# First transfers of an attention and feed-forward kernel chained one behind the other, with the first stage's order changed on all engines

## The chip, the cores and the metric

The chip is a Trainium2. The program handles one batch entry of 2048 tokens on one core; the input has eight entries, so the same program runs on the chip's eight cores at once, each with its own copy of the weights to load. The metric is the device time of the slowest core in microseconds.

## The reference

```python
xn = _layernorm(x)                                   # x: [8, 2048, 1024]
qkv = xn @ W_attn + b_attn                           # 16 heads of 64
att = q @ k.T / sqrt(64) / temperature + alibi_bias  # causal
y = softmax(att) @ v;  attn = y @ W_proj + b_proj
gate, up = xn @ wg.T, xn @ wu.T                      # hidden size 3072, int32 weights / 127
ffn = (silu(gate) * up) @ wd.T
out = x + attn + ffn
```

## The kernel before

The work has three parts: a first stage that normalises x, transposes it and makes V and the first head pair's q and k; a long middle stage (attention woven with gate and up); and the output stage. The change touches the first and a few waits around it.

x has 16 tiles of 128 tokens. For tile i, SP loads it into one of four buffers `xstage` (lines 339 to 343; from the fifth tile on it waits until the tile that held the buffer is normalised, semaphore `v_xn`). The vector engine takes statistics (two `bn_stats` and a `bn_aggr`, line 499), ScalarE the square root `sd` (line 624), the vector engine the reciprocal `rs` and the normalised tile `xn_st` (line 507). PE transposes it with eight 128-column matmuls into PSUM, in turn `ps_s` and `ps_gu` (line 742). ScalarE copies that to `xnT` (line 631). Below, Ti is the transpose of tile i and xi the tile itself.

A V unit is one tile times one half of the V weights: eight matmuls of 512 columns from `xnT` and `wv_b` into one of two halves of `ps_t` (line 767), copied by ScalarE to `Vt` (line 639). There are 32 units, numbered here in PE's order: V0, V1 and so on. The table `v_at` sets that order: half 0 of the first four tiles, then half 1 of the same four, then both halves of each tile. A q or k group is eight matmuls of 512 columns for four tiles (line 707). q of head pair 0 is taken from `ps_m` by the vector engine (`evac_q`, line 474), k from `ps_y` by ScalarE (`evac_k`, line 600). The loop index i of each engine's stream carries several tiles at once: PE transposes tile i and makes V of tile i-1; ScalarE takes the root of tile i, copies the transposed tile i-2 and V of tile i-3.

The orders are written out by hand per engine, with semaphores between engines. Transfers go through two queues: x on SP's (q1), weights that are cast from float32 or int32 to bf16 while they move on POOL's (q0). POOL waits for x0 and x1, then issues the V weights of half 0 (2 MB read), the weights of the first q/k pair (1 MB) and the V weights of half 1 (2 MB) without a wait between them (lines 403 to 409), then runs twelve memsets for constant rows of `qx` and `kx` (lines 410 to 418). After the twelfth tile is normalised it issues the first gate and up weights, the next pair's q/k weights and W_proj.

Of the kernel before, what the change touches and what calls it, by code (L numbers as in the profile page):

```python
# [11 lines left out]
I32 = mybir.dt.int32  # L12
# [7 lines left out]
DC = C // 128  # L20
# [25 lines left out]
    "v_t", "v_cbq", "v_ln", "v_xn", "v_q", "v_mx", "v_mc", "v_rc", "v_y", "v_h", "v_out",  # L46
# [101 lines left out]
def build_program(T):  # L148
    NT = T // 128
# [26 lines left out]
    with st:  # L176
# [93 lines left out]
        v_at = {i: [(i - 1, 0)] for i in range(1, 5)}  # L270
        v_at[4] += [(tt, 1) for tt in range(4)]
        for i in range(5, NT + 1):
            v_at[i] = [(i - 1, 0), (i - 1, 1)]
        V0 = {i: sum(len(v_at[k]) for k in v_at if k < i) for i in range(NT + 3)}
# [40 lines left out]
        def _(e):  # L315
# [34 lines left out]
            for k, (_, t, _, M) in enumerate(steps):  # L350
                if M is not None and M[0] == "qk" and M[2]:
                    p, u = M[1] // 8 + 1, M[1] % 8
                    if u == 0:
                        if p >= 2:
# [37 lines left out]
        def _(e):  # L392
# [29 lines left out]
            cast_qk(1)  # L422
            e.dma_start(out=wpj_b[:, :], in_=wproj_r[:, :]).then_inc(sem["l_wp"], 16)
# [45 lines left out]
        def _(e):  # L469
# [21 lines left out]
            for i in range(NT + 1):  # L491
                if i < NT:
                    b = i % 4
                    e.wait_ge(sem[f"l_x{b}"], 16 * (i // 4 + 1))
                    for k in range(2):
                        e.bn_stats(st6[b][:, 6 * k:6 * k + 6], xstage[b][:, k * 512:(k + 1) * 512]).then_inc(  # L496
                            sem["v_ln"], 1)
                    e.wait_ge(sem["v_ln"], 4 * i + 1 if i else 2)
                    e.bn_aggr(mv[b][:, :], st6[b][:, :]).then_inc(sem["v_ln"], 1)
                if i:  # L500
                    b = (i - 1) % 4
                    e.wait_ge(sem["a_sd"], i)
                    e.reciprocal(rs[b][:, :], sd[b][:, :]).then_inc(sem["v_ln"], 1)
                    e.wait_ge(sem["v_ln"], 4 * i + (3 if i < NT else 0))
                    if i > 4:
                        e.wait_ge(sem["p_xT"], i - 4)
                    e.tensor_scalar(xn_st[b][:, :], xstage[b][:, :], mv[b][:, 0:1], rs[b][:, :],
                                    AluOpType.subtract, AluOpType.mult).then_inc(sem["v_xn"], 1)
                if i == 1:
                    e.wait_ge(sem["l_const"], 16 * 4)  # L510
                    e.tensor_scalar(t8_s[0:1, :], temp_s[0:1, :], 8.0, None, AluOpType.mult).then_inc(
                        sem["v_t"], 1)
                    e.wait_ge(sem["v_t"], 2)
                    e.reciprocal(c11_s[0:1, :], t8_s[0:1, :]).then_inc(sem["v_t"], 1)
                if i == 5:
                    e.wait_ge(sem["a_c"], 1)
                    e.tensor_scalar(cbq_s[:, :], bqk_s[:, 0:8], cvec_s[:, :], None, AluOpType.mult).then_inc(
                        sem["v_cbq"], 1)
                    e.wait_ge(sem["v_cbq"], 1)
                if i >= 6 and i % 4 == 2:  # L520
                    evac_q(0, i // 4 - 1)
# [73 lines left out]
        def _(e):  # L595
# [21 lines left out]
            e.wait_ge(sem["v_t"], 1)  # L617

            V3 = Vt.rearrange("p (g d) -> p g d", d=VW)
            for i in range(NT + 3):  # L620
                if i < NT:
                    b = i % 4
                    e.wait_ge(sem["v_ln"], 4 * i + 2 if i else 3)
                    e.activation(sd[b][:, :], mv[b][:, 1:2], AF.Sqrt, bias=eps_s[:, :]).then_inc(sem["a_sd"], 1)
                if i == 4:
                    e.wait_ge(sem["p_c"], 1)
                    e.activation(cvec_s[:, :], ps_m[:, 0:1], AF.Copy).then_inc(sem["a_c"], 1)
                if 2 <= i < NT + 2:
                    k = i - 2
                    e.wait_ge(sem["p_xT"], k + 1)  # L630
                    e.activation(xT3[:, :, k * 128:(k + 1) * 128],
                                 (ps_gu if k % 2 else ps_s).rearrange("p (d t) -> p d t", d=DC),
                                 AF.Copy).then_inc(sem["a_xe"], 1)
                for x, (tt, half) in enumerate(v_at.get(i - 2, [])):
                    n = V0[i - 2] + x
# [6 lines left out]
                    if i == 6 and x == 0:  # L642
                        evac_k(0, 0)
                if i >= 11 and i % 4 == 3:
                    evac_k(0, i // 4 - 1)
# [55 lines left out]
        def _(e):  # L701
# [33 lines left out]
            e.wait_ge(sem["l_id"], 16)  # L735
            for i in range(NT + 2):
                if i < NT:
                    e.wait_ge(sem["v_xn"], i + 1)
                    if i >= 2:
                        e.wait_ge(sem["a_xe"], i - 1)  # L740
                    for dc in range(DC):
                        mm = e.matmul((ps_gu if i % 2 else ps_s)[:, dc * 128:dc * 128 + 128],
                                      xn_st[i % 4][:, dc * 128:(dc + 1) * 128], ident_s[:, :],
                                      start=(dc % 4 == 0), stop=(dc % 4 == 3))
                    mm.then_inc(sem["p_xT"], 1)
                if i == 3:
                    e.wait_ge(sem["v_t"], 3)
                    e.wait_ge(sem["l_const"], 16 * 4)
                    e.matmul(ps_m[:, 0:1], onesf_s[0:1, :], c11_s[0:1, :], start=True, stop=True).then_inc(
                        sem["p_c"], 1)  # L750
                for x, (tt, half) in enumerate(v_at.get(i, [])):
                    n = V0[i] + x
                    e.wait_ge(sem["a_xe"], tt + 1)
                    if i == 1:
                        e.wait_ge(sem["l_wv0"], 16)
                    if i == 4 and x == 1:

                        e.wait_ge(sem["a_xe"], 4)
                        e.wait_ge(sem["l_wq0"], 16)
                        e.wait_ge(sem["a_c"], 1)  # L760
                        q_or_k(0, 0, ps_m, range(DC)).then_inc(sem["p_qk"], 1)
                        q_or_k(0, 1, ps_y, range(DC)).then_inc(sem["p_qk"], 1)
                        e.wait_ge(sem["l_wv1"], 16)
                    if n >= 2:
                        e.wait_ge(sem["a_v"], n - 1)
                    for dc in range(DC):
                        mm = e.matmul(ps_t[:, n % 2 * 512:n % 2 * 512 + 512],  # L767
# [224 lines left out]
```

## Time and profile before

| | us |
|---|---|
| runs of the kernel | 1156.03, 1156.49, 1157.23; median 1156.49 |
| profiled execution, device time | 1156.21 |
| its span (slowest core, core 4) | 1154.7 |
| spans of the eight cores | 1150.5 to 1154.7 |
| first gate/up matmul of core 4 | 113.88 |

The profile was taken on the slowest core. The span goes from the first to the last instruction; the device time also holds what lies around it (1.5 us). Times inside are from the span's start. A row of the chain of waits says how long the end of the program hung on that piece; a row of the timeline says when an instruction or a run of like ones started, how long it took, and in brackets how long its engine had been idle and who released it. PE is the matmul engine, DVE the vector engine, ACT ScalarE, POOL GpSimd.

### The profile page before, as it was taken

Reading aid. Unit: us, or ns where it says so; the run is one execution under the profiler, and the core shown is the slowest. Engines: PE = TensorE matmul, PEld = TensorE weight load, DVE = VectorE, ACT = ScalarE, POOL = GpSimd, SP = SyncE. Lnnn points to the kernel's source line nnn. Section 1 sums busy time; section 2 is a strip of 40 time slices with the busy share of each in tenths; the row PEclk is TensorE's granted clock in tenths of the full one; section 3 lists DMA queues with packets and bytes.
Section 4 is the critical chain, followed back from the end, with each engine's and each line's share of the span. In section 5 each row is a group of like instructions: output and inputs, shape, how many; then the busy total and the mean of one; then the engine's idle time right before and its main releaser. Section 6 shows DMA issues by size and latency. Waiting matters only on the chain.

```text
span 1154.7 us, 24726 instructions; the slowest of 8 cores (1150.5 to 1154.7 us)
## 1 busy us (share of the span) xinstructions
PE 1107.8 (96%) x7830; PEld 569.8 (49%) x7830; DVE 586.5 (51%) x1190; ACT 531.3 (46%) x965; POOL 267.2 (23%) x289
## 2 busy tenths in 40 slices
PE   2898999999999999999999999999999999999998
PEld 1344455555555555555555555555555344444443
DVE  5441866766666766676666666666773100000110
ACT  1443456655755665565566566556667300000000
POOL 7210122222221222122222112112223432121221
PEclk9899999999999999999999999999999999999999
DMA  9439041333312333133311312112420652525222
GB/s 188 126 95 179 12 80 41 75 66 70 74 29 62 78 62 65 38 74 67 69 38 24 67 33 52 31 31 56 165 56 20 217 189 73 182 73 182 73 73 73
DMA packets 39648, 94.19 MB, mean 82 GB/s; under 512 B 5876, under 2 KB 26485, under 8 KB 38438
## 3 DMA queue, kind: packets, MB, share of 16 engines
q0 software_dynamic: 7872, 35.66, 16.1%
q1 hardware_dynamic: 28770, 48.45, 13.5%
q10 hardware_dynamic: 2884, 8.50, 1.9%
q8 instruction: 71, 1.16, 0.4%
q14 instruction: 51, 0.42, 0.1%
HBM read 90.49 MB, written 27.26 MB: 102 GB/s over the span
## 4 chain that ended last, share of the span: by engine, by line
PE 88%; DVE 5%; issue 3%; DMA 2%; ACT 1%; POOL 1%; DVEq 0%; ACTq 0%; POOLq 0%; SPq 0%
PE ps_gu L727 25%; PE ps_dn L895 14%; PE ps_s L818 10%; PE ps_t L799 10%; PE ps_m L707 9%; PE ps_y L834 5%; PE ps_dn L890 5%; PE ps_t L767 5%; DVE cm L548 3%; DMA xstage<-xin 2%; PE ps_m L847 1%; PE ps_s L821 1%; PE ps_t L803 1%; PE ps_m L855 1%; DVE st L496 1%
## 5 line engine op out<-in xcount | busy, mean ns | idle before, releaser
L548 DVE TENSOR_REDUCE cm<-ps_s 128x1 f32<-128x512 f32 (+3 forms) x640 | 380.1, 608 | 198.5 <-PE ps_s L818 105.0
L656 ACT ACTIVATE pt<-ps_t 128x512 bf16<-128x512 f32 (+1 forms) x576 | 327.3, 575 | 222.3 <-PE ps_t L799 134.2
L727 PE MATMUL ps_gu<-xnT,wubuf 128*128 128x512 bf16 x768 | 261.9, 378 | 2.1 <-DVE hst L484 1.7
L727 PE MATMUL ps_gu<-xnT,wgbuf 128*128 128x512 bf16 x768 | 261.3, 378 | 1.2 <-ACT kst L600 1.2
L818 PE MATMUL ps_s<-kx,qx 67*128 67x512 bf16 (+3 forms) x640 | 213.1, 347 | 10.4 <-DVE cm L548 9.1
L799 PE MATMUL ps_t<-qx,kx 98*128 98x512 bf16 (+3 forms) x640 | 216.4, 348 | 1.5 <-ACT pt L656 1.2
L426 POOL TENSOR_SCALAR th_s<-th_s 128x512 f32<-128x512 f32 x96 | 59.4, 618 | 626.0 <-ACT th_s L608 626.0
L895 PE MATMUL ps_dn<-wdres,hb 128*128 128x512 bf16 x768 | 168.5, 379 | 0.0
L834 PEld LDWEIGHTS ps_y<-Vt,pt 128*128 128x128 bf16 x2176 | 125.4, 97 | 82.0 <-issue 0.4
L834 PE MATMUL ps_y<-Vt,pt 128*128 128x65 bf16 x2176 | 138.9, 193 | 0.0
L589 DVE SCALAR_TENSOR_TENSOR outsb<-ps_dn,xres 128x512 f32<-128x512 f32 x32 | 20.7, 687 | 205.3 <-PE ps_dn L895 205.3
L707 PE MATMUL ps_m<-xnT,wqk_b 128*128 128x512 bf16 x480 | 122.9, 380 | 0.0
L895 PEld LDWEIGHTS ps_dn<-wdres,hb 128*128 128x128 bf16 x768 | 75.2, 98 | 90.6
L432 POOL TENSOR_TENSOR gs_s<-th_s,gh_s 128x512 bf16<-128x512 f32 x96 | 111.0, 1156 | 26.4 <-POOL th_s L426 26.4
L818 PEld LDWEIGHTS ps_s<-kx,qx 67*128 67x128 bf16 x640 | 61.8, 97 | 94.3 <-issue 41.3
L727 PEld LDWEIGHTS ps_gu<-xnT,wubuf 128*128 128x128 bf16 x768 | 73.0, 98 | 57.4 <-issue 5.8
L727 PEld LDWEIGHTS ps_gu<-xnT,wgbuf 128*128 128x128 bf16 x768 | 73.5, 98 | 52.7 <-issue 1.7
L484 DVE SCALAR_TENSOR_TENSOR hst<-ps_gu,gs_s 128x512 bf16<-128x512 f32 x96 | 65.7, 684 | 41.4 <-POOL gs_s L432 31.3
L799 PEld LDWEIGHTS ps_t<-qx,kx 98*128 98x128 bf16 x640 | 62.5, 98 | 30.5 <-issue 5.1
L608 ACT ACTIVATE th_s<-ps_gu 128x512 f32<-128x512 f32 x96 | 57.1, 595 | 29.5 <-PE ps_gu L727 28.9
L767 PE MATMUL ps_t<-wv_b,xnT 128*128 128x512 bf16 x256 | 62.2, 399 | 4.2 <-DMA wv_b<-wv_r 2.7
L707 PEld LDWEIGHTS ps_m<-xnT,wqk_b 128*128 128x128 bf16 x480 | 41.8, 98 | 38.9 <-issue 1.2
(77 smaller groups left out, 793.1 us busy)
## 6 DMA issues: line engine op xcount, KB each, us to landing
h_sc<-hst SPq DMA_DIRECT2D x96, 128.0 KB, 1.7
hb<-h_sc SPq DMA_DIRECT2D x4, 3072.0 KB, 14.1
xstage<-xin SPq DMA_DIRECT2D x16, 512.0 KB, 6.3
xres<-xin POOLq DMA_DIRECT2D x16, 512.0 KB, 4.6
out<-outsb ACTq DMA_DIRECT2D x15, 512.0 KB, 2.7
wgbuf<-wg_r POOLq DMA_DIRECT2D x12, 512.0 KB, 6.4
wubuf<-wu_r POOLq DMA_DIRECT2D x12, 512.0 KB, 9.1
wd_sc<-wd_r POOLq DMA_DIRECT2D x12, 512.0 KB, 8.3
```

Source lines behind the costliest of these rows:

```text
L426: e.tensor_scalar(th_s[f % 2][:, :], th_s[f % 2][:, :], 1.0, 1.0, AluOpType.add, AluOpType.mult).then_inc(sem["g_th"], 1)
L432: e.tensor_tensor(gs_s[f % 2][:, :], th_s[f % 2][:, :], gh_s[f % 2][:, :], AluOpType.mult).then_inc(sem["g_s"], 1)
L484: e.scalar_tensor_tensor(hst[f % 4][:, :], ps_gu[:, 512:1024], 1.0 / 127.0, gs_s[f % 2][:, :], AluOpType.mult, AluOpType.mult).then_inc(se ...
L548: e.tensor_reduce(cm[:, c0:c0 + 1], ps_s[:, s % 2 * 512:s % 2 * 512 + w], AX.X, AluOpType.max, negate=True).then_inc(sem["v_mx"], 1)
L656: e.activation(pt[t % NPT][:, 0:w], ps_t[:, t % 2 * 512:t % 2 * 512 + w], AF.Exp).then_inc(sem["a_e"], 1)
L707: mm = e.matmul(ps[:, :], wqk_b[p % 2][:, f0 + dc * 256:f0 + dc * 256 + 128], xnT[:, dc * T + tc * 512:dc * T + (tc + 1) * 512], start=(dc ...
L727: mm = e.matmul(ps_gu[:, r // 8 * 512:r // 8 * 512 + 512], w[:, w0:w0 + 128], xnT[:, dc * T + tb * 512:dc * T + tb * 512 + 512], start=(dc ...
L767: mm = e.matmul(ps_t[:, n % 2 * 512:n % 2 * 512 + 512], xnT[:, dc * T + tt * 128:dc * T + (tt + 1) * 128], wv_b[:, half * 4096 + dc * 512: ...
L799: mm = e.matmul(ps_t[:, c0 + off:c0 + off + w], k_[0:KT, kt * 128:(kt + 1) * 128], q_[0:KT, b * 512 + i0 * 128:(b + 1) * 512], start=(x == ...
L818: mm = e.matmul(ps_s[:, r0:r0 + w], q_[0:KS, b * 512 + i * 128:b * 512 + (i + 1) * 128], k_[0:KS, c0:c0 + w], start=True, stop=not diag)
L834: mm = e.matmul(ps_y[:, i * VW:(i + 1) * VW], pt[a % NPT][:, c0:c0 + 128], Vt[:, (kt * H + h) * VW:(kt * H + h + 1) * VW], start=(T0[n] == ...
L895: return e.matmul(ps_dn[:, r0:r0 + 512], hb[tb % 2][:, hc * 512 + ts * 128:hc * 512 + ts * 128 + 128], wdres[:, hc * 1024 + half * 512:hc ...
```

## The change

SP issues x0 and x1 at once, x2 and x3 when the first quarter of the V weights (`l_wva`) has landed, x4 when x2 has landed, x5 when x4 has landed, x6 when all V weights have landed, and the rest as before. POOL fills the constant rows of pair 0 first, now written as 32-bit words, half as many elements; it issues the first quarter of the V weights after x0, the second after x1, the q/k weights after the second quarter has landed, the third quarter after x3, the fourth after the q/k weights. The memsets for pair 1 go behind the weight transfers after the twelfth tile. V units are taken in another order (half 0 of six tiles, half 1 of the same six, then both halves tile by tile), q/k groups and transposes stand elsewhere, and ScalarE runs a root on a constant ahead of its first real one. The vector engine's single counter `v_ln` becomes three.

```diff
@@ sync @@
             for i in range(NT):
+                if i == 2:
+                    e.wait_ge(sem["l_wva"], 16)
+                if i == 4:
+                    e.wait_ge(sem["l_x2"], 16)
+                if i == 5:
+                    e.wait_ge(sem["l_x0"], 32)
+                if i == 6:
+                    e.wait_ge(sem["l_wv1"], 32)
                 if i >= 4:
                     e.wait_ge(sem["v_xn"], i - 3)
                 e.dma_start(out=xstage[i % 4][:, :], in_=xin[i * 128:(i + 1) * 128, :]).then_inc(
                     sem[f"l_x{i % 4}"], 16)
-            e.wait_ge(sem["g_set"], 13)
+            e.wait_ge(sem["g_set"], 7)
@@ gpsimd @@
+            def set_rows(q, k):
+                for j in range(2):
+                    e.wait_ge(sem["g_set"], k + 3 * j)
+                    e.memset(qx[q][j][64:96, :].bitcast(I32), 0x3F803F80).then_inc(sem["g_set"], 1)
+                    e.wait_ge(sem["g_set"], k + 3 * j + 1)
+                    e.memset(kx[q][j][64:96, :].bitcast(I32), 0).then_inc(sem["g_set"], 1)
+                    e.wait_ge(sem["g_set"], k + 3 * j + 2)
+                    e.memset(kx[q][j][96:98, :].bitcast(I32), 0x3F803F80).then_inc(sem["g_set"], 1)
             e.memset(Vt.rearrange("p (g d) -> p g d", d=VW)[:, :, 64:65], 1.0).then_inc(sem["g_set"], 1)
+            set_rows(0, 1)
             e.wait_ge(sem["l_x0"], 16)
+            e.dma_start(out=wv_b[:, 0:2048], in_=wv_r[0, :, 0:2048]).then_inc(sem["l_wva"], 16)
             e.wait_ge(sem["l_x1"], 16)
-            for half in range(2):
-                e.dma_start(out=wv_b[:, half * 4096:(half + 1) * 4096], in_=wv_r[half, :, :]).then_inc(
-                    sem[f"l_wv{half}"], 16)
-                if half == 0:
-                    cast_qk(0)
...
+            e.dma_start(out=wv_b[:, 2048:4096], in_=wv_r[0, :, 2048:4096]).then_inc(sem["l_wvb"], 16)
+            e.wait_ge(sem["l_wvb"], 16)
+            cast_qk(0)
+            e.wait_ge(sem["l_x3"], 16)
+            e.dma_start(out=wv_b[:, 4096:6144], in_=wv_r[1, :, 0:2048]).then_inc(sem["l_wv1"], 16)
+            e.wait_ge(sem["l_wq0"], 16)
+            e.dma_start(out=wv_b[:, 6144:8192], in_=wv_r[1, :, 2048:4096]).then_inc(sem["l_wv1"], 16)
             e.wait_ge(sem["v_xn"], NT - 4)
             cast_gu(0)
             cast_gu(1)
             cast_qk(1)
+            set_rows(1, 7)
+            e.wait_ge(sem["g_set"], 13)
             e.dma_start(out=wpj_b[:, :], in_=wproj_r[:, :]).then_inc(sem["l_wp"], 16)
@@ vector, from tile 6 on @@
+            for i in range(6, NT):
+                if i + 1 < NT:
+                    statistics(i + 1)
+                normalise(i)
+                if i % 4 == 1:
                     evac_q(0, i // 4 - 1)
             evac_q(0, NTB - 1)
@@ scalar @@
             e.wait_ge(sem["v_t"], 1)
+            e.activation(sd[3][:, :], eps_s[:, :], AF.Sqrt)
...
+            for i in range(6, NT):
+                if i + 1 < NT:
+                    evac_x(i + 1)
+                evac_v(2 * i, 2 * i + 1)
+                if i + 2 < NT:
+                    deviation(i + 2)
+                evac_v(2 * i + 1, 2 * i + 2)
+                if i % 4 == 0:
                     evac_k(0, i // 4 - 1)
@@ tensor @@
+            transpose_x(0)
+            transpose_x(1)
+            values(0, 2)
+            transpose_x(2)
+            transpose_x(3)
...
+            values(2, 4)
+            first_qk(0)
+            transpose_x(4)
+            transpose_x(5)
+            values(4, 6)
+            e.wait_ge(sem["l_wv1"], 32)
+            values(6, 10)
+            transpose_x(6)
+            values(10, 12)
+            for i in range(6, NT):
+                if i + 1 < NT:
+                    transpose_x(i + 1)
+                values(2 * i, 2 * i + 2)
+                if i % 4 == 3:
+                    first_qk(i // 4)
```

**PE, first stage.** `wv_b` is the V weights, `ident_s` the transposing identity, `wqk_b` the q/k weights. A row is a run of like matmuls with their count; eight on `ps_t` are one V unit. Before, from T1 to the first four units of half 1:

```order
L742 MATMUL ps_gu<-ident_s,xn_st 128x128 x8
L767 MATMUL ps_t<-wv_b,xnT 128x512 x8
L742 MATMUL ps_s<-ident_s,xn_st 128x128 x8
L767 MATMUL ps_t<-wv_b,xnT 128x512 x8
L742 MATMUL ps_gu<-ident_s,xn_st 128x128 x8
L749 MATMUL ps_m<-c_s,onesf_s 128x1
L767 MATMUL ps_t<-wv_b,xnT 128x512 x8
L742 MATMUL ps_s<-ident_s,xn_st 128x128 x8
L767 MATMUL ps_t<-wv_b,xnT 128x512 x8
L707 MATMUL ps_m<-xnT,wqk_b 128x512 x8
L707 MATMUL ps_y<-xnT,wqk_b 128x512 x8
L767 MATMUL ps_t<-wv_b,xnT 128x512 x32
```

And now:

```order
L804 MATMUL ps_gu<-ident_s,xn_st 128x128 x8
L820 MATMUL ps_t<-wv_b,xnT 128x512 x16
L804 MATMUL ps_s<-ident_s,xn_st 128x128 x8
L804 MATMUL ps_gu<-ident_s,xn_st 128x128 x8
L846 MATMUL ps_m<-c_s,onesf_s 128x1
L820 MATMUL ps_t<-wv_b,xnT 128x512 x16
L771 MATMUL ps_m<-xnT,wqk_b 128x512 x8
L771 MATMUL ps_y<-xnT,wqk_b 128x512 x8
L804 MATMUL ps_s<-ident_s,xn_st 128x128 x8
L804 MATMUL ps_gu<-ident_s,xn_st 128x128 x8
L820 MATMUL ps_t<-wv_b,xnT 128x512 x48
```

Transposes now come in twos with two units behind them, T4 and T5 stand behind the first q/k groups, and six units follow these without a break; the wait for the second half's weights has moved from the fifth unit to the seventh.

**POOL, start of the program.** Before:

```order
L402 MEMSET Vt 128x256
L406 DMA wv_b<-wv_r 128x4096 [waits l_x0,l_x1]
L395 DMA wqk_b<-wqk_r 128x2048
L406 DMA wv_b<-wv_r 128x4096
L414 MEMSET qx 32x2048 [waits g_set]
L416 MEMSET kx 32x2048 [waits g_set]
L418 MEMSET kx 2x2048 [waits g_set]
```

Now:

```order
L422 MEMSET Vt 128x256
L416 MEMSET qx 32x1024 [waits g_set]
L418 MEMSET kx 32x1024 [waits g_set]
L420 MEMSET kx 2x1024 [waits g_set]
L425 DMA wv_b<-wv_r 128x2048 [waits l_x0]
L427 DMA wv_b<-wv_r 128x2048 [waits l_x1]
L405 DMA wqk_b<-wqk_r 128x2048 [waits l_wvb]
L431 DMA wv_b<-wv_r 128x2048 [waits l_x3]
L433 DMA wv_b<-wv_r 128x2048 [waits l_wq0]
```

Six memsets moved ahead of the first weight transfer and are half as long, and each later weight transfer waits for an earlier transfer.

**ACT, the loop from tile 6 on.** Before, one turn of the loop and the next:

```order
L624 ACTIVATE sd<-mv,eps_s 128x1 [waits v_ln]
L631 ACTIVATE xnT<-ps_s 128x8x128 [waits p_xT]
L639 ACTIVATE Vt<-ps_t 128x8x64 [waits p_v] x2
L624 ACTIVATE sd<-mv,eps_s 128x1 [waits v_ln]
L631 ACTIVATE xnT<-ps_gu 128x8x128 [waits p_xT]
L639 ACTIVATE Vt<-ps_t 128x8x64 [waits p_v] x2
```

Now:

```order
L663 ACTIVATE xnT<-ps_gu 128x8x128 [waits p_xT]
L673 ACTIVATE Vt<-ps_t 128x8x64 [waits p_v]
L658 ACTIVATE sd<-mv,eps_s 128x1 [waits v_ag]
L673 ACTIVATE Vt<-ps_t 128x8x64 [waits p_v]
L663 ACTIVATE xnT<-ps_s 128x8x128 [waits p_xT]
L673 ACTIVATE Vt<-ps_t 128x8x64 [waits p_v]
L658 ACTIVATE sd<-mv,eps_s 128x1 [waits v_ag]
L673 ACTIVATE Vt<-ps_t 128x8x64 [waits p_v]
```

The root (L658, before L624) stood ahead of the copy of a transposed tile and of both V copies; now it stands between the two V copies.

## Rows read from the trace of the kernel before

**Rows 1.** The page, busy time per engine: us, share of the span, instructions.

```profile
PE 1107.8 (96%) x7830; PEld 569.8 (49%) x7830; DVE 586.5 (51%) x1190; ACT 531.3 (46%) x965; POOL 267.2 (23%) x289
```

**Rows 2.** Chain that ended last, 0 to 110 us: start, us, what.

```profile
1.06 5.73 DMA xstage<-xin
...
17.23 14.70 DMA xstage<-xin
...
44.31 6.91 PE ps_t L767 x32
51.22 0.45 PE ps_gu L742 x8
51.67 3.45 PE ps_t L767 x16
```

**Rows 3.** Timeline of PE: start us, us, what, count [idle before, releaser].

```profile
21.00 3.42 PE L767 MATMUL ps_t<-wv_b,xnT 128*128 128x512 bf16 x8 [2.69 <-DMA wv_b<-wv_r]
...
76.17 0.61 PE L742 MATMUL ps_s<-ident_s,xn_st 128*128 128x128 bf16 x8 [2.00 <-ACT xnT L631]
...
113.88 0.38 PE L727 MATMUL ps_gu<-xnT,wgbuf 128*128 128x512 bf16 x1 [1.25 <-ACT kst L600]
```

**Rows 4.** Timeline of POOL, first 15 us.

```profile
2.26 1.25 POOL L402 MEMSET Vt<- 128x256 bf16 x1
...
8.95 0.54 POOL L406 DMA_DIRECT2D wv_b<-wv_r  x1 [5.45 <-DMA xstage<-xin]
...
10.60 1.80 POOL L414 MEMSET qx<- 32x2048 bf16 x1
...
14.80 1.80 POOL L418 MEMSET kx<- 2x2048 bf16 x1
```

**Rows 5.** Timeline of DVE and ACT: one tile beside memsets, then a steady turn.

```profile
10.53 2.42 DVE L507 TENSOR_SCALAR xn_st<-xstage,mv,rs 128x1024 bf16<-128x1024 f32 x1
...
51.32 0.60 ACT L639 ACTIVATE Vt<-ps_t 128x512 bf16<-128x512 f32 x1 [1.13 <-PE ps_t L767]
...
51.81 0.29 ACT L624 ACTIVATE sd<-mv,eps_s 128x1 f32<-128x1 f32 x1
...
52.20 0.16 DVE L503 RECIPROCAL rs<-sd 128x1 f32<-128x1 f32 x1 [4.63 <-ACT sd L624]
52.54 0.81 DVE L507 TENSOR_SCALAR xn_st<-xstage,mv,rs 128x1024 bf16<-128x1024 f32 x1 [0.18 <-DVE rs L503]
53.27 1.28 DVE L496 BATCH_NORM_STATS2 st<-xstage 128x6 f32<-128x512 f32 x2
...
54.65 0.21 DVE L499 BATCH_NORM_AGGREGATE mv<-st 128x2 f32<-128x12 f32 x1
```

**Rows 6.** Tiles: x from 10 to 22 us, x from 36 to 62 us, wgbuf throughout.

```profile
L342 SPq DMA_DIRECT2D xstage<-xin x3: 327/328/328, 13.0 to 19.7; - x3
...
DMA to landing us min/median/max: 10.8/14.7/14.8
...
DMA to landing us min/median/max: 3.4/3.4/3.7
...
DMA to landing us min/median/max: 6.0/6.4/15.0
```

**Rows 7.** DMA queues, 0 to 60 us: packets, MB, share of 16 engines.

```profile
q1 hardware_dynamic: 1838, 6.74, 34.8%
q0 software_dynamic: 576, 2.62, 29.7%
```

**Rows 8.** Windows: PE, PEld, DVE, ACT, POOL busy, granted clock, DMA share, GB/s.

```profile
21.00:24.50 3.50, 3.50 (x13) 1.37 (x14) 0.54 (x1) 0.00 (x0) 3.26 (x3) 1.00 1.15 224
30.00:34.00 4.00, 2.94 (x8) 0.89 (x8) 1.48 (x4) 0.54 (x2) 3.76 (x3) 0.62 0.89 279
```

**Rows 9.** Spans and granted clock of cores.

```profile
core 0: 1150.5 us, clock 0.998
...
core 4: 1154.7 us, clock 0.995
```

More of the change, by code:

```diff
@@ L267, in gu_of @@
             return (f // 4, f % 4) if f < NF_ATT else (f // 8 * 2 + f % 2, f % 8 // 2)
[L270 to L274, printed above, removed]
+        v_units = [(tt, 0) for tt in range(6)] + [(tt, 1) for tt in range(6)]
+        v_units += [(tt, half) for tt in range(6, NT) for half in range(2)]
         FM = [NF_ATT * 16 * (k + 1) // len(steps) for k in range(len(steps))]
@@ L353, in _ @@
                     if u == 0:
[L354 removed]
+                        if p == 1:
+                            e.wait_ge(sem["g_set"], 13)
+                        else:
                             e.wait_ge(sem["p_t"], pair_done(p - 2))
@@ L489, in _ @@
             e.memset(nm[1][:, :], 0.0).then_inc(sem["v_t"], 1)
[L491 to L520, printed above, removed]
@@ L617, in _, with deviation, evac_x, evac_v @@
             e.wait_ge(sem["v_t"], 1)
+            e.activation(sd[3][:, :], eps_s[:, :], AF.Sqrt)
             V3 = Vt.rearrange("p (g d) -> p g d", d=VW)
[L620 to L635, printed above, removed]
+            def deviation(i):
+                e.wait_ge(sem["v_ag"], i + 1)
+                e.activation(sd[i % 4][:, :], mv[i % 4][:, 1:2], AF.Sqrt, bias=eps_s[:, :]).then_inc(
+                    sem["a_sd"], 1)
+            def evac_x(i):
+                e.wait_ge(sem["p_xT"], i + 1)
+                e.activation(xT3[:, :, i * 128:(i + 1) * 128],
+                             (ps_gu if i % 2 else ps_s).rearrange("p (d t) -> p d t", d=DC),
+                             AF.Copy).then_inc(sem["a_xe"], 1)
+            def evac_v(n0, n1):
+                for n in range(n0, n1):
+                    tt, half = v_units[n]
                     e.wait_ge(sem["p_v"], n + 1)
@@ L641, in _ @@
                                  AF.Copy).then_inc(sem["a_v"], 1)
-                    if i == 6 and x == 0:
-                        evac_k(0, 0)
-                if i >= 11 and i % 4 == 3:
+            deviation(0)
+            deviation(1)
+            evac_x(0)
+            evac_x(1)
+            deviation(2)
+            evac_v(0, 1)
+            deviation(3)
+            evac_v(1, 2)
+            evac_x(2)
+            evac_x(3)
+            e.wait_ge(sem["p_c"], 1)
+            e.activation(cvec_s[:, :], ps_m[:, 0:1], AF.Copy).then_inc(sem["a_c"], 1)
+            evac_v(2, 4)
+            deviation(4)
+            evac_k(0, 0)
+            deviation(5)
+            evac_x(4)
+            evac_x(5)
+            evac_v(4, 9)
+            deviation(6)
+            evac_v(9, 10)
+            deviation(7)
+            evac_x(6)
+            evac_v(10, 12)
+            for i in range(6, NT):
[6 more added lines that the diff above has]
+                if i % 4 == 0:
                     evac_k(0, i // 4 - 1)
@@ L733, in gate_up, with transpose_x, values @@
                         mm.then_inc(sem["p_u"], 1)
[L735 to L752, printed above, removed]
-                    e.wait_ge(sem["a_xe"], tt + 1)
[L754 to L763, printed above, removed]
+            def transpose_x(i):
+                e.wait_ge(sem["v_xn"], i + 1)
+                if i >= 2:
+                    e.wait_ge(sem["a_xe"], i - 1)
+                for dc in range(DC):
+                    mm = e.matmul((ps_gu if i % 2 else ps_s)[:, dc * 128:dc * 128 + 128],
+                                  xn_st[i % 4][:, dc * 128:(dc + 1) * 128], ident_s[:, :],
+                                  start=(dc % 4 == 0), stop=(dc % 4 == 3))
+                mm.then_inc(sem["p_xT"], 1)
+            def values(n0, n1):
+                for n in range(n0, n1):
+                    tt, half = v_units[n]
+                    e.wait_ge(sem["a_xe"], tt + 1)
                     if n >= 2:
```

75 lines of the change are left out of this document (60 added, 15 removed), and 2 rows, old and new, of the table SEMS.

## The prediction

> **What bounds the kernel now.** I began with the busy shares: PE works 96% of the span, everything else about half [rows 1]. A saving must therefore shorten PE's path, and the change touches only the first stage (layer norm, transposes, V, first q/k pair). So I next read the chain that ended last, for that stage alone [rows 2]. Until 44.3 us it hops from a transfer of x to the vector engine to a few matmuls; the piece of 14.70 us waits for one tile of x. From 44.31 us it is nearly all PE: eight matmuls of a V unit take 1.73 us (3.45 for two), eight transposes 0.45. The timeline of PE [rows 3] has the rest: the first V unit waits for its weights until 21.00 us, PE stops for 2.00 us at 76.17 (and again at 97.58), and the first gate/up matmul, where the next stage begins, starts at 113.88 us. That instant is my yardstick: the 1040.8 us behind it keep their order on every engine, so I move the end by as much as the yardstick moves.
>
> The work ahead of it is 16 transposes, 32 V units and 8 q or k groups: 16 x 0.45 + 40 x 1.73 = 76.4 us. PE is thus without useful full-speed work for 37.5 us. Before 44.31 it did only 5 transposes, 4 V units and 2 groups (12.6 us). From there 11 transposes, 28 units and 6 groups are left, 63.8 us; with two stops of 2.0 that is 67.8, against 68.3 to the end of the last group. I keep the 0.5 as friction. The last group is followed by 1.25 us of waiting for its copy.
>
> **Part 1, POOL: memsets first, weights in parts.** The row initialisation for the first head pair (6 memsets) now stands ahead of the first weight transfer. Vt's memset ends at 3.51. A memset of 2048 bf16 values costs 1.8 us whether it covers 32 partitions or 2 [rows 4], so the price goes by the length of a row, and the new ones write rows of 1024 words. The trace has no word memset: by elements it is 0.9 us, by bytes 1.8. I take 0.9, as the cost per element of the nearest row, plus 0.11 for the step between two: 6 x 1.01 = 6.1, so the first weights are issued at 9.6 us instead of 8.95 (with bytes: at 15.0). The Trainium skill ("VectorE: DVE Perf Modes", section "Zero memsets can be issued as uint32 (trn2)") says a memset costs a cycle per element whatever the type; it says so of the vector engine only, and no row here shows it for POOL. Beside POOL's memsets the normalising pass took 2.42 us against 0.81 [rows 5]; now its first two fall after them. The activation table's load also leaves the chain. So both first tiles are transposed by about 13.5 us, but PE then waits for weights anyway: this gains nothing.
>
> **Part 2, the transfers.** Prices: a 512 KB tile of x alone lands 3.4 us after issue, but 10.8 to 14.8 us after it with the weight queue full; a transfer of a weight part's size (1 MB read, 512 KB written) lands 6.0 to 6.4 us after issue [rows 6]. Engine time: queue q1 moved 6.74 MB in 34.8% of 60 us, so a tile costs 1.63 us; queue q0 wrote 2.62 MB in 29.7%, so a part costs 3.56 us [rows 7]. Behind weights tile 4 landed at 13.0 + 10.8 = 23.8, tile 5 at 17.2 + 14.7 = 31.9: 8.1 us for 1.63 us of work, so x gets about 0.2 of the engines there. Of a part's 6.2 us, 2.6 are not engine time; half before the data, half behind, I get: wva lands at 15.9; wvb 19.7; x2 (issued at 16.0) 20.9; x3 23.6; wq0 27; x4 31.8; wv1 complete 35.2; x5 (issued when x4 has landed) 36.4; x6 39. In total the engines are no less busy than before, but about 3 us are lost between x1 and wva.
>
> **What the chain costs.** A lone tile's 3.4 us less its 1.63 leaves 1.8 us per link, exposed only where the other queue is empty. The Trainium skill ("DMA: Bandwidth & Descriptors", section "Anatomy of one DMA") speaks against chaining: about 2.0 us fixed per transfer, mostly the receipt. By 2.0 in place of 1.8, four links (wva, x2, x4, x5) would be 0.8 us dearer.
>
> **Part 3, PE's order.** From landing to transpose: statistics 1.38, aggregate and hop 0.30, sd to rs 0.39, rs to xn 0.34, xn 0.81, hop 0.13: 3.35 us [rows 5]. x2 (20.9) is normalised by 24.1, x3 behind it by 27.3; T3 runs at 27.4 and V2 behind it and the small product for the temperature at 28.3. The first matmuls after idling run 512 columns in 427 ns, the lower level of 1.2 GHz, though the granted clock of that stretch reads 1.00; later the grant itself fell to 0.62 after PE had idled [rows 3, 8]. I charge V2 3.4 us: V2 to 31.7, V3 33.4, q and k 36.9, T4 37.35. T5 waits for x5: 36.4 + 3.35 = **39.75**. Then T5 0.45 and V4 to V9 10.4: 50.6 us. The first unit that needs wv1, V6, comes at 43.7, and wv1 is there at 35.2.
>
> **Part 4, the steady loop.** Removed: both stops of 2.00 us, since the vector engine now takes q out of PSUM after the norm that PE needs. Added: ACT's square root for tile i+2 stands behind the copy of V unit 2i. From the end of that unit: copy starts 0.10 later (51.22 to 51.32), sd 0.49 later, rs 0.39, xn 0.34 + 0.81, hop 0.14 = 2.27 us [rows 2, 5]; PE has only the unit of 1.73 to cover it. So T6, T8, T10, T11, T12, T14, T15 come 0.54 us late (T9 and T13 have q/k groups as cover, T7 two more units): 7 x 0.54 = 3.8. The bounds are 0 (copy and root overlap better) and 7 x 0.8. The second pair's six memsets now run beside tiles 12 and 13, whose normalising may take 2.4 instead of 0.8; 13 is covered, I charge 1.0 (0 to 1.6).
>
> **Sum.** 50.6 + 0.54 (T6) + ten transposes, 22 units, 6 groups 52.9 + six late transposes 3.2 + memsets 1.0 + friction 0.5 + 1.25 = **110.0 us**, against 113.88: 3.9 us less. The profiled execution took 1156.21 us (span 1154.7), 0.28 below the median of the runs; 1156.2 - 3.9 gives 1152.3, and **1152.4** beside the median. A difference below 0.2% (2.3 us) can't be told from none. The cheap parts together: sources of statistics split over three semaphores, the earlier waits for 7 instead of 13, and the wpj load behind memsets cost nothing: the work that waits on them is tens of us away.
>
> **Rivals.**
> A. *The late transposes don't happen.* ACT's copy and root overlap, and x5's link is shorter by about 1 us. For it: after a copy the root starts before the copy's end [rows 5]. Against it: my 2.27 already has that overlap. It would give 110.0 - 3.8 - 1 = 105.2, or 1147.6.
> B. *Memsets cost by bytes.* Weights are issued at 15.0, 5.4 us later, and wva gates x2 and all behind: 115.4, or 1157.7, no change. The same comes out if the slowest core is set otherwise: the spans reach from 1150.5 to 1154.7 us [rows 9], and a core with a low grant early on could give back the 3.9.
> C. *Slower: x4 and x5 in series behind weights.* x5 is issued only when x4 has landed. The yardstick is x5's landing plus 73.6, so from a landing after 42.6 us on the kernel is measurably slower. If x4 takes the 14.7 us that a tile took behind a full weight queue [rows 6], it lands at 35.7, and x5 at its own 8.1 lands at 44: 117.6, or 1159.9. For it: the row. Against it: wv1's last part should be through by 35 us, after which a tile takes 3.4.
> D. *The change doesn't start earlier*: all of the gain would vanish if T2 to V3 ran at the low clock throughout; 3.5 more gives 1156.
>
> **Chances.** Forecast 0.48 (own range 1149 to 1154.1), A 0.22, B 0.12, C 0.10, D 0.08. Faster: the forecast and A, with a little of B and D, 0.72; same 0.18; slower 0.10. The range takes in nearly all of A and all of B, and leaves C out: 1146.6 to 1158.0.
>
> **What the new profile would show.** Right: the first weight transfer issued at 9 to 10 us, word memsets of about 0.9 us; x3 landing at 23 to 24, T5 near 40, wv1 waited for by nobody; no stop of 2.0 us beside q/k groups, but transposes of the loop waiting about 0.5 us for xn; the first gate/up matmul near 110. Wrong: memsets of 1.8 us (B); tiles four and five taking over 8 us each (C); PE without a wait between V units from 50 us on (A).

## The result, and the profile after

The changed kernel takes 1159.80 us (median of 7 runs, 1159.53 to 1160.92), the kernel before, run beside it, 1156.58. The ratio is 1.0030 with a 95% interval of 1.0019 to 1.0041: slower by about 3.4 us, where 4 us less had been forecast. The profiled execution took 1159.6 us. Now and then an execution of any of these kernels runs at a lower granted clock on one die and takes longer; the ratios leave those out.

Cores, of the changed kernel:

```profile
core 1: 1154.7 us, clock 0.997
...
core 4: 1158.0 us, clock 0.998
```

All eight spans lie between these two; before they went from 1150.5 to 1154.7 [rows 9]. So it is not one unlucky core. One execution of each kernel is profiled, on all eight cores; where nothing else is said, lines are those of its slowest core (core 4 for both kernels).

The yardstick, and what PE waited for, in the timeline of PE (start us, us, what [idle before, releaser]):

```profile
17.80 1.86 PE L820 MATMUL ps_t<-wv_b,xnT 128*128 128x512 bf16 x4 [4.85 <-DMA wv_b<-wv_r]
24.92 5.28 PE L820 MATMUL ps_t<-wv_b,xnT 128*128 128x512 bf16 x12 [5.26 <-DMA wv_b<-wv_r]
...
46.06 0.61 PE L804 MATMUL ps_gu<-ident_s,xn_st 128*128 128x128 bf16 x8 [3.23 <-DVE xn_st L525]
...
66.44 0.61 PE L804 MATMUL ps_s<-ident_s,xn_st 128*128 128x128 bf16 x8 [0.73 <-DVE xn_st L525]
...
117.66 0.38 PE L791 MATMUL ps_gu<-xnT,wgbuf 128*128 128x512 bf16 x1 [1.25 <-ACT kst L634]
```

The first gate/up matmul, the forecast's yardstick, starts at 117.66 instead of 113.88 us [rows 3]; the 1040.3 us behind it are as long as before (1040.8). So the yardstick held and everything is decided in the first stage. The half unit at 17.80 and the rest at 24.92 wait for the two weight parts; T5 starts at 46.06, where 39.75 was forecast.

The chain that ended last, for the first 60 us (start, us, what):

```profile
2.27 1.26 POOL Vt L422
...
3.64 0.96 POOL qx L416
...
9.86 7.80 DMA wv_b<-wv_r
17.70 0.04 issue
17.74 8.30 DMA xstage<-xin
...
26.17 6.12 DMA xstage<-xin
...
32.41 10.00 DMA xstage<-xin
...
42.50 1.30 DVE st L512 x2
```

Before, the chain ran through one tile of x (14.70 us) [rows 2]. Now it is POOL's memsets, then four transfers in series, wva, x2, x4, x5, 32.2 us together. Nothing but waits holds them in that order. How busy the transfer engines were (columns: PE, PEld, DVE, ACT, POOL busy, granted clock, DMA share, GB/s):

```profile
6.00:12.00 6.00, 1.08 (x10) 0.87 (x11) 3.78 (x11) 0.71 (x3) 4.92 (x6) 1.00 0.16 23
12.00:24.00 12.00, 2.81 (x12) 1.11 (x12) 0.09 (x1) 1.93 (x2) 0.00 (x0) 1.00 0.96 157
24.00:27.00 3.00, 2.08 (x5) 0.74 (x6) 0.87 (x2) 0.00 (x0) 0.53 (x1) 1.00 0.34 74
27.00:39.00 12.00, 10.19 (x44) 4.71 (x43) 5.71 (x13) 4.16 (x8) 1.06 (x2) 0.86 0.98 177
```

wva and wvb are the first and second part of the first half of the V weights. There are two holes: from 6 to 12 us the share is 0.16, because x0 and x1 have landed and POOL is still at its memsets (5.0 us of the engines unused); from 24 to 27 it is 0.34, because the q/k weights wait for wvb and x4 for x2, and both land at nearly the same time (2.0 us). The clock plays no part in either: the grant is 1.00, as it was in the first 30 us before.

The memsets, and the loop's turn from the copy of a V unit on:

```profile
3.64 0.94 POOL L416 MEMSET qx<- 32x1024 int32 x1
...
86.34 0.94 POOL L416 MEMSET qx<- 32x1024 int32 x1
87.41 1.38 POOL L418 MEMSET kx<- 32x1024 int32 x1
```

```profile
61.65 0.61 PE L804 MATMUL ps_gu<-ident_s,xn_st 128*128 128x128 bf16 x8
...
64.08 0.60 ACT L673 ACTIVATE Vt<-ps_t 128x512 bf16<-128x512 f32 x1 [0.66 <-PE ps_t L820]
64.58 0.28 ACT L658 ACTIVATE sd<-mv,eps_s 128x1 f32<-128x1 f32 x1
64.97 0.16 DVE L520 RECIPROCAL rs<-sd 128x1 f32<-128x1 f32 x1 [3.33 <-ACT sd L658]
65.38 0.81 DVE L525 TENSOR_SCALAR xn_st<-xstage,mv,rs 128x1024 bf16<-128x1024 f32 x1 [0.25 <-DVE rs L520]
```

The words cost by elements, 0.94 against 1.80 us [rows 4]; why the one at 87.41 took 1.38 is not explained; it ran beside the normalising of tile 12 (87.09 to 87.90). In the loop the root waits for the copy of V12, as forecast, and T8 follows at 66.44, 4.79 us behind T7 where a turn without a stop takes 3.90.

### The profile page after: what moved, and what is told of

Its sections match the earlier page's. It is cut to its first block, busy times and chain, and to the rows that moved or that the text cites. A ratio compares the mean times of both kernels' runs of the same rounds, so it can differ in the third digit from the quotient of the medians.

```text
span 1158.0 us, 24758 instructions; the slowest of 8 cores (1154.7 to 1158.0 us)
## 1 busy us (share of the span) xinstructions
PE 1108.6 (96%) x7830; PEld 569.5 (49%) x7830; DVE 582.1 (50%) x1190; ACT 532.8 (46%) x966; POOL 257.5 (22%) x291
## 4 chain that ended last, share of the span: by engine, by line
PE 87%; DVE 5%; issue 3%; DMA 3%; POOL 1%; ACT 1%; DVEq 0%; ACTq 0%; POOLq 0%; SPq 0%
PE ps_gu L791 25%; PE ps_dn L980 14%; PE ps_s L903 10%; PE ps_t L884 10%; PE ps_m L771 9%; PE ps_y L919 5%; PE ps_dn L975 5%; PE ps_t L820 3%; DVE cm L582 2%; DMA xstage<-xin 2%; PE ps_m L932 1%; PE ps_s L906 1%; PE ps_t L888 1%; DMA wv_b<-wv_r 1%; PE ps_m L940 1%
## 5 line engine op out<-in xcount | busy, mean ns | idle before, releaser
L642 ACT ACTIVATE th_s<-ps_gu 128x512 f32<-128x512 f32 x96 | 57.1, 595 | 29.4 <-PE ps_gu L791 28.9
```

## The experiments

Each time stands beside runs of the kernel before on the same chip, so the ratios compare. "First gate/up" is the mean over the eight cores of the yardstick in the profiled execution, for cores of one execution differ by 2 to 6 us. It is split at T6, for ten V units and the first q/k groups lie ahead of it in every kernel: the mean start of T6, and the mean time from there to the first gate/up matmul.

| kernel | median us | ratio to before (95%) | first gate/up, mean | T6, mean | from T6 on, mean |
|---|---|---|---|---|---|
| before | 1156.58 | | 111.4 | 51.3 | 60.2 |
| changed | 1159.80 | 1.0030 (1.0019 to 1.0041) | 116.1 | 56.2 | 60.0 |
| root first | 1152.86 | 0.9976 (0.9966 to 0.9986) | 109.2 | 54.6 | 54.6 |
| memsets later | 1154.59 | 0.9991 (0.9981 to 1.0001) | 110.8 | 50.8 | 59.9 |
| x unchained | 1155.59 | 1.0004 (0.9994 to 1.0015) | 113.0 | 53.1 | 60.0 |
| x and weights unchained | 1155.19 | 0.9997 (0.9986 to 1.0007) | 112.3 | 52.3 | 59.9 |
| only x2 and x3 unchained | 1154.57 | 0.9985 (0.9975 to 0.9994) | 111.2 | 51.2 | 60.0 |
| bf16 memsets | 1165.52 | 1.0081 (1.0067 to 1.0094) | 122.1 | 61.3 | 60.8 |
| root first + memsets later | 1147.98 | 0.9933 (0.9920 to 0.9946) | 104.5 | 49.9 | 54.6 |
| the same, x unchained | 1147.80 | 0.9930 (0.9917 to 0.9943) | 104.5 | 49.9 | 54.6 |
| the same as root first + memsets later, V4 ahead of T5 | 1148.34 | 0.9932 (0.9919 to 0.9945) | 104.1 | 49.5 | 54.6 |
| before, chained transfers | 1163.47 | 1.0068 (1.0052 to 1.0084) | 120.0 | 60.0 | 60.0 |
| before, q out one turn later | 1150.40 | 0.9952 (0.9939 to 0.9965) | 104.6 | 50.4 | 54.2 |

On the mean core the whole loss lies ahead of T6, which starts 4.9 us later; the part from T6 on is as long as before. It lost its two stops and gained six late transposes, and these come to the same.

Theory 1, formed from the two traces: two terms that have nothing to do with each other. The chain memsets, wva, x2, x4, x5 sets T5, and the loop behind it has seven late transposes.

**Root first.**

```diff
@@ scalar, loop from tile 6 on (and likewise deviation(6) ahead of the copy of V8) @@
-                evac_v(2 * i, 2 * i + 1)
                 if i + 2 < NT:
                     deviation(i + 2)
-                evac_v(2 * i + 1, 2 * i + 2)
+                evac_v(2 * i, 2 * i + 2)
```

> The changed kernel with one edit: ScalarE takes the square root of tile i+2 ahead of the copy of V unit 2i (and that of tile 6 ahead of the copy of V8), so the normalised tile is ready when PE comes to its transpose. Theory 1 (the loop's late transposes are worth what the profile of the changed kernel shows: seven stops of 0.72 to 1.10 us, 5.4 us together): the seven stops go, the first gate/up matmul moves from 117.7 to about 112.3 us, the time to about 1154.4. Rival (the loop is bound by something else next, such as x tiles or the V copies, and the stops reappear under another name): less than 2 us gained, 1158 or more.

The ratio falls by 0.0054, 6.2 us, the mean yardstick by 6.9. Its timeline around the same turn:

```profile
61.89 0.30 ACT L658 ACTIVATE sd<-mv,eps_s 128x1 f32<-128x1 f32 x1
...
62.66 0.60 ACT L673 ACTIVATE Vt<-ps_t 128x512 bf16<-128x512 f32 x1 [0.48 <-PE ps_t L819]
64.13 0.61 PE L803 MATMUL ps_s<-ident_s,xn_st 128*128 128x128 bf16 x8
```

T8 comes 3.90 us behind T7 (60.23) and waits for nothing. The gain is more than the 5.4 us of idle time that the seven stops showed. The starts say why: a late turn takes 4.79 instead of 3.90, 0.89 us for an idle time of 0.73, and the one beside the second memsets 5.17. Six times 0.89 and once 1.27 are 6.6 us; two of the seven transposes still come 0.20 us late here (79.49 stands 4.10 behind 75.39), which leaves 6.2. Of the mean yardstick's 6.9 the rest is a T5 that started 1.1 us earlier on the mean core, on which this edit has no hold, less some 0.4 us at a lower clock behind it.

**Memsets later.**

```diff
             e.memset(Vt..., 1.0).then_inc(sem["g_set"], 1)
-            set_rows(0, 1)
             e.wait_ge(sem["l_x0"], 16)
...
             e.dma_start(out=wv_b[:, 2048:4096], ...).then_inc(sem["l_wvb"], 16)
+            set_rows(0, 1)
             e.wait_ge(sem["l_wvb"], 16)
```

> The changed kernel with pair 0's six memsets moved from ahead of the first weight transfer to behind the issue of the second. Theory 1 (the end hangs on the chain memsets, wva, x2, x4, x5): wva is issued when x0 has landed, at about 4.9 instead of 9.9 us, wvb at about 8; x5 lands 3 to 5 us earlier (37.5 to 39.5), the first gate/up matmul at 113 to 115, time 1155 to 1157. Rival (the transfer engines as a whole are the limit, not their order): wvb and x2 take longer by what wva is earlier, x5 lands within 1 us of 42.4, time 1159 or more.

4.5 us by the ratio, 5.3 by the mean yardstick. Its chain on the slowest core:

```profile
6.59 6.65 DMA wv_b<-wv_r
...
13.31 5.47 DMA xstage<-xin
...
18.92 8.18 DMA xstage<-xin
...
27.22 8.82 DMA xstage<-xin
```

The same four links, begun 3.3 us earlier, and x5 lands at 36.0 instead of 42.4: the transfers don't catch up, they gain more than the earlier start, for the links are shorter too (29.1 us together instead of 32.2). T5 starts 6.4 us earlier than in the changed kernel, but the first gate/up matmul only 4.7 (112.97). The 1.7 between them are in the six V units behind T5, 12.21 us here and 10.52 in the changed kernel, and the granted clock (the column ahead of the DMA share) was 0.87 there:

```profile
40.15 12.21 PE L820 MATMUL ps_t<-wv_b,xnT 128*128 128x512 bf16 x48
...
40.00:53.00 13.00, 12.36 (x54) 5.15 (x51) 3.66 (x9) 4.75 (x9) 0.00 (x0) 0.87 0.21 83
```

This happens on 3 of the 8 cores here and, wholly or in part, on 4 in the changed kernel, each time behind PE's wait for T5. Which cores it strikes these runs don't explain (core 4 of the changed kernel waited 3.23 us and kept 1.00).

**bf16 memsets**, the same question from the other side:

```diff
-                    e.memset(qx[q][j][64:96, :].bitcast(I32), 0x3F803F80).then_inc(sem["g_set"], 1)
+                    e.memset(qx[q][j][64:96, :], 1.0).then_inc(sem["g_set"], 1)
```

(and so for the two on `kx`).

> The changed kernel with its memsets written as bf16 again, twice the elements, in the same places. Theory 1 (the chain memsets, wva, x2, x4, x5 sets the end, at 1 us per us): six memsets of 1.9 instead of 1.06 us issue wva at about 15 instead of 9.9 us, first gate/up matmul 5 us later, time 1164 to 1166. Rival (a fixed amount of transfer work sets the end; the transfers catch up): 1161 or less.

```profile
3.64 1.80 POOL L416 MEMSET qx<- 32x2048 bf16 x1
...
15.73 0.54 POOL L425 DMA_DIRECT2D wv_b<-wv_r  x1
```

5.9 us more for a first issue 5.9 us later (15.73 against 9.86). That looks like one for one, but is so by chance: on the mean core T5 comes 4.4 us later, the units behind it take 0.8 more, and the part from T6 on 0.85 more, for the edit writes pair 1's memsets as bf16 too, and T12, beside them, waits 1.5 instead of 0.7 us on every core. The forecast's rival B had priced this case at "no change" against the kernel before; it is 9.4 us.

**x unchained, all unchained, only x2 and x3 unchained.** The first takes out SP's four waits, the second also POOL's waits for wvb, x3 and the q/k weights, the third only this one:

```diff
-                if i == 2:
-                    e.wait_ge(sem["l_wva"], 16)
```

> The changed kernel without SP's four waits on transfers (x2 for wva, x4 for x2, x5 for x4, x6 for wv1); POOL's waits stay. Theory 1 (the serial links x2, x4, x5 set the end): x2 and x3 land by 12 us while POOL is still at its memsets, x4 and x5 well before 35; the weights come a few us earlier or equal; first gate/up matmul 3 to 8 us earlier, time 1152 to 1157. Rival (without the chain x takes engines from the weights that PE waits for first): wva and wvb land later than 17.7 and 24.9, time 1160 or more.

> As the run without SP's waits on transfers, and POOL too issues the weight parts without waiting for earlier transfers (only x0 and x1): the changed order of work with the old way of loading. Theory 1: close to the run with x alone unchained, within 1.5 us, because the weight queue is first in, first out either way; q/k weights land by about 28, wv1 by 35. Rival (chaining of the weights protects x2 to x5 from the full weight queue, as the 10.8 to 14.8 us per tile of the kernel before suggested): x4 and x5 land past 30 us, and the time is 2 us or more worse than with the weights chained.

> The changed kernel without the one wait of x2 (and so x3) for wva; the waits of x4 for x2, x5 for x4 and x6 for wv1 stay. Theory 1 (what the chain cost was the stretch from 6 to 12 us in which the transfer engines stood nearly idle behind POOL's memsets, and x2 and x3 fill it): as good as with all four waits gone, 1155 to 1156.5. Rival (x4 and x5 in series are the costly links): x2 and x3 early don't help, 1158.5 or more.

By the ratios the three gain 3.0, 3.8 and 5.2 us against the changed kernel. The third is the telling one: with x4, x5 and x6 still chained it is at least as good as with every wait gone, so x4 and x5 in series are not what costs once x2 and x3 are free. What went is the first hole. Window of 6 to 12 us, x2 and x3 unchained:

```profile
6.00:12.00 6.00, 1.01 (x8) 0.77 (x8) 4.74 (x10) 0.59 (x2) 5.07 (x6) 1.00 0.78 231
```

The share is 0.78 instead of 0.16. The rival's fear, x taking engines from the weights, is there: on the mean core PE waits for wvb until 23.4 us with x unchained and 21.5 with the chain (21.9 with x2 and x3 free), 1.9 us later. Unchaining the weights too (rival: tiles would take 10 us and more behind them) cost nothing measurable: tiles did take up to 10.6 us, but PE does not need x4 and x5 before it is through with V0 to V3 and q, k.

What T5 then waits for is no transfer. In these three runs, and in the fourth without SP's waits below, it starts 6.55 us behind the first q group on every core. The vector engine takes q out of PSUM before it comes to the statistics of tile 5. From the fourth, the vector engine and then PE:

```profile
34.16 0.81 DVE L483 TENSOR_SCALAR qst<-ps_m,cvec_s,cbq_s 128x512 bf16<-128x512 f32 x1
34.88 1.28 DVE L504 BATCH_NORM_STATS2 st<-xstage 128x6 f32<-128x512 f32 x2
...
38.43 0.61 PE L795 MATMUL ps_gu<-ident_s,xn_st 128*128 128x128 bf16 x8 [2.49 <-DVE xn_st L517]
```

So the changed order holds a stop of 2.5 us that no transfer can remove. Taking q out behind the statistics of tile 5 was not tried.

**Root first + memsets later**, then the same without SP's waits.

> The changed kernel with both single edits together: square root ahead of the V copy, and pair 0's memsets behind the first two weight issues. Theory 1 (two separate terms, the loop's seven stops and the late start of the chain): they add; the runs with one edit gave 6.9 and 5.2 us against the changed kernel, so the first gate/up matmul of the slowest core at 106 to 108 and 1147.5 to 1149 us, faster than both kernels. Rival (both edits relieve the same wait): the sum is clearly less than 12, 1151 or more.

> The kernel with both edits, and without SP's four waits on transfers. Rival first (the chain's serial links x2, x4, x5 still set T5): x4 and x5 land before 30 us, T5 is no longer late, 2 to 4 us faster than with the chain. Theory 1 (once the weights start early the chain and the full queues are worth the same, since the first unit needs wvb and x2 with x3 then take engines from it): wvb lands 2 to 4 us later than 17, the first unit ends later by as much, T5 earlier; time within 1.5 us of the run with both edits.

The two edits add: 6.2 + 4.5 = 10.7 expected by the single runs, 11.2 measured, and the result is 7.7 us faster than the kernel before. Unchained it is the same within the interval. Chains of the two (chained, then unchained):

```profile
6.76 6.81 DMA wv_b<-wv_r
...
13.65 4.97 DMA xstage<-xin
...
18.75 7.09 DMA xstage<-xin
...
25.97 9.41 DMA xstage<-xin
```

```profile
1.50 7.21 DMA xstage<-xin
...
9.24 12.27 DMA wv_b<-wv_r
```

With the chain PE waits for T5 (39.04 us), without it for wvb (21.64 instead of 17.45), and T5 starts at 38.43. So chaining first transfers was worth nothing in either form here; it did harm only where it left the engines idle.

**V4 ahead of T5.**

```diff
             transpose_x(4)
+            values(4, 5)
             transpose_x(5)
-            values(4, 6)
+            values(5, 6)
```

> The kernel with both edits (root ahead of the V copy, memsets behind the first two weight issues), and V4 moved ahead of the transpose of tile 5 on PE, with ScalarE's copies in the order that this needs. Theory 1: PE waits 3.7 us for tile 5 in that kernel; a unit of 1.73 us now runs inside the wait, so 1.5 to 1.9 us less, 1146.0 to 1146.5. Rival (the wait is only moved, since V5 onwards needs tile 5 or wv1 anyway): within 0.5 us of 1148.0.

ScalarE's copies follow the same order. A miss: no gain, though the unit does run inside the wait. The timeline of PE:

```profile
38.38 1.89 PE L820 MATMUL ps_t<-wv_b,xnT 128*128 128x512 bf16 x8 [1.50 <-ACT xnT L663]
40.16 0.61 PE L804 MATMUL ps_gu<-ident_s,xn_st 128*128 128x128 bf16 x8
42.13 1.02 PE L820 MATMUL ps_t<-wv_b,xnT 128*128 128x512 bf16 x4 [1.37 <-ACT xnT L663]
```

V4 waits 1.50 us for ScalarE's copy of T4, and V5, which now follows T5 directly, 1.37 for the copy of T5, which V4 had covered. The mean yardstick is 0.4 lower (104.1 against 104.5), but no more than a stretch at the lower clock behind T5 accounts for it, which three cores had without this edit (1.7 us each) and none has with it; the time shows nothing.

**Before with the chained transfers.** PE's, the vector engine's and ScalarE's order stay; SP's and POOL's transfers and memsets of the first stage are those of the changed kernel.

```diff
@@ tensor, the first V unit and the fifth @@
-                        e.wait_ge(sem["l_wv0"], 16)
+                        e.wait_ge(sem["l_wva"], 16)
+                        e.wait_ge(sem["l_wvb"], 16)
...
-                        e.wait_ge(sem["l_wv1"], 16)
+                        e.wait_ge(sem["l_wv1"], 32)
```

> The kernel before with only the transfers of the change (SP's waits, weights in parts, POOL's order with word memsets first); PE, the vector engine and ScalarE keep the old order. Theory 1 (order must follow the landing): ScalarE takes the root of tile 2 ahead of copying the first transposed tile, so the first V unit waits for x2 (22 to 26 us) and starts at 26 to 30 instead of 21; V units of half 1 wait for wv1 at 39; first gate/up matmul at 119 to 125, time 1161 to 1168. Rival (the transfers alone are harmless, the new order of work is what costs): within 2 us of 1156.

7.9 us slower than before. The first transposed tile is copied only behind the root of tile 2:

```profile
23.77 0.29 ACT L636 ACTIVATE sd<-mv,eps_s 128x1 f32<-128x1 f32 x1 [14.45 <-DVE rs L515]
...
23.97 1.00 ACT L643 ACTIVATE xnT<-ps_s 128x1024 bf16<-128x1024 f32 x1
```

and PE's first unit starts at 25.60. So the new transfers cost 7.9 us under the old order of work, part of it by this copy's place (on the mean core PE starts V0 at 25.5 us, where in the changed kernel wvb is there at 21.5), and the new order takes back more than half.

**Before, q out one turn later.**

```diff
@@ vector @@
-                if i >= 6 and i % 4 == 2:
+                if i >= 7 and i % 4 == 3:
                     evac_q(0, i // 4 - 1)
```

> The kernel before with one edit: the vector engine takes each middle q group out of PSUM one turn later, behind the statistics and the normalising that PE waits for. Theory 1 (each of the two stops of 2.00 us goes, nothing else moves): 4.0 us less, the first gate/up matmul of the slowest core at about 110, time 1152.0 to 1152.8. Rival (the stop moves to the next tile or to the k group): less than 2 us.

5.6 us by the ratio, with one condition changed. Both stops are gone:

```profile
71.74 0.61 PE L742 MATMUL ps_s<-ident_s,xn_st 128*128 128x128 bf16 x8
72.19 3.62 PE L767 MATMUL ps_t<-wv_b,xnT 128*128 128x512 bf16 x16
```

No bracket stands behind T10. That it is more than 4.0 has the same cause as above: from the k group at 72.28 to T10 at 76.17 went 3.89 us before and 1.73 now (70.01 to 71.74), 2.16 for an idle time of 2.00, and the first unit behind the stop stood 0.19 farther from T10 than it does now. That makes 4.7 us for two. The rest is the clock. In the kernel before, on six of the eight cores, the two units behind one of the two stops took 5.30 instead of 3.62 us; the grant in windows of 7 or 8 us around them was 0.76 to 0.79. Core 5:

```profile
91.97 0.61 PE L742 MATMUL ps_s<-ident_s,xn_st 128*128 128x128 bf16 x8 [2.00 <-ACT xnT L631]
92.60 5.30 PE L767 MATMUL ps_t<-wv_b,xnT 128*128 128x512 bf16 x16
```

Without the stops no core has such a stretch. On the mean core that is 1.26 us; with 4.7 it is the 5.96 by which the part from T6 on is shorter here (60.18 and 54.22). Core 4, the slowest, from which the forecast was read, was one of the two that were spared. Behind the stops of 0.72 us in the changed kernel's loop no core fell.

## Why the prediction was wrong

The sign was wrong, the range missed the time by 1.8 us, and 0.10 had been given to slower. Point by point:

- **Yardstick and work behind T5: right.** From T5 to the first gate/up matmul are 0.45 + 10.4 + 52.9 + 1.25 = 65.0 us of work and the last wait; with the 6.6 us of late turns this gives 71.6, and the trace has 117.66 - 46.06 = 71.6. The forecast's "friction" of 0.5 was part of the 0.7 of the two stops that their idle time doesn't show.
- **Part 1, the memsets: right in size** (0.94 for 0.9, first issue at 9.86 for 9.6). By elements, as the Trainium skill ("VectorE: DVE Perf Modes", section "Zero memsets can be issued as uint32 (trn2)") has it for the vector engine, the trace agrees for POOL. **Wrong in weight.** The sum compared the new issue with the old one (8.95), which waited for x1. It did not ask what the memsets cost against a first weight transfer that needs x0 alone, and x0, no longer sharing the queue with x2 and x3, landed at 4.8 us instead of 6.8. The note that "about 3 us are lost between x1 and wva" was 5.0 us of the engines.
- **Part 2, the landings: this is the step that failed.** Forecast and measured on the slowest core: wva 15.9 and 17.7, wvb 19.7 and 24.9, x2 20.9 and 26.0, x4 31.8 and 32.3, x5 36.4 and 42.4. Three things in it. The shares: I had given x a fifth of the engines beside weights, by rows from a full weight queue; when only wvb was left and x2 and x3 were issued together, the three finished within some 2.5 us of one another, so wvb, which PE needed first, came 5 us late. The chains of the two queues met: both waited at 24 to 27 us, a hole that a sum with one queue always full can't have. And every weight behind wvb moved with it (the last part was issued at 31.24, x5 at 32.41), so x5 ran beside them and took 10.0 us instead of 4.6. T5 at 46.06 instead of 39.75 is 6.3 of the 7.7 us between 110.0 and 117.66. Core 4 is the extreme here: on the mean core wvb came at 21.5 and T5 at 43.7, 1.8 and 4.0 us behind the forecast.
- **The chain's fixed price.** By rows a lone link cost 1.8 us more than its bytes. That did not matter beside what the links ran against: 6.1 to 10.0 us for 1.63 us of work. The Trainium skill ("DMA: Bandwidth & Descriptors", section "Anatomy of one DMA") has about 2.0 us for it; the section is on transfers that GpSimd issues, of the four links wva alone, and no run here isolates the price.
- **Part 4, the loop: mechanism right, size off.** The same transposes that were named came late, and the stops beside the q/k groups were gone. A late transpose was priced at 0.54 and measured 0.89. The path that I had at 2.27 us takes 2.61, counted from the start of the next unit (63.83 for V13): the copy begins 0.25 behind it, where I had 0.10 by counting from the modelled end in the chain (51.22; T5 itself started at 51.06), rs to xn is 0.41 for 0.34, and the end of xn to T8 0.25 for 0.14. The seven cost 6.6 us where 3.8 stood, beyond the bound of 5.6; the memsets' part, charged 1.0, was 0.4 of it. On core 4 the trade is 4.7 removed for 6.6 added, so there the loop alone is 1.9 us slower; on the mean core the two stops had cost 6.0 with the clock, and it is 0.7.
- **The rivals.** C was right in its sign and about its threshold (x5 after 42.6 us; it landed at 42.4, with the dearer loop enough for +3.4). That it also hit the figures, 117.6 and 1159.9, is luck: x5 landed 1.6 us earlier than C had it, and what lies behind was 1.6 dearer. It was wrong in its place: x4 took 6.1 us, not 14.7, and the late landing began with POOL's memsets and wvb. Taking x4 and x5 out of the series gains nothing once x2 and x3 are free. A has no late transposes, but they came; B has memsets by bytes, and they went by elements; D's low clock through V3 (16 matmuls in 5.31 us at 33.62) was there in part but had no say, for T5 then waited 3.23 us for x5.

## What to carry to other kernels

In a start-up that hangs on transfers, ask of every wait that is put between them what the transfer engines do meanwhile: filling the window of 6 to 12 us with its share of 0.16 took away all of the chain's harm that these runs could measure, and work that only fills constants belongs behind the first issue, not ahead of it. Count a stop in a loop by the distance of two starts, not by the idle time, and check where a short instruction that others wait for (here a square root of 0.3 us) stands in its engine's order. An edit of that size was worth as much as the best edit to the transfers (5.2 us): 5.6 us on the kernel before, 6.2 on the changed one. And read more than the slowest core: the one that the forecast was taken from had been spared the clock's part of the stops.

## What was not expected of the hardware

- The idle time that the profile gives ahead of a PE instruction understates what the stop costs: 0.89 us per turn for 0.73, 2.35 for 2.00. In each stop 0.17 of it lies in how a run's end is modelled: sixteen matmuls stand as 3.62 us, and the next run starts 3.45 us behind their start (58.20 and 61.65).
- A stop of 2.00 us cost six of eight cores another 1.68 us behind it, at a granted clock of 0.76 to 0.79 in the windows around; behind stops of 0.72 us no core lost anything.
- Whether splitting the V weights costs anything in itself no run isolates. Queue q0 needed 864 packets for the same 2.62 MB instead of 576, at 28.5 to 33.6% of 60 us in the runs with parts (the changed kernel has the highest) against 29.4 and 29.7% without.
- One and the same link, 512 KB of x, took from 5.0 to 10.0 us in these chains, with different transfers beside it; which of two queues yields to which was not settled by these runs.
